# Layer norm roots by one power instruction on GpSimd in place of ten DVE steps, in a gated two-layer mixture kernel

## What is computed

```
def _layernorm(x, eps=1e-05):
    m = jnp.mean(x, axis=-1, keepdims=True)
    v = jnp.var(x, axis=-1, keepdims=True)
    return (x - m) / jnp.sqrt(v + eps)

x = x + tanh(g_xattn) * xattn(_layernorm(x), token_ids, ctx)   # 4 experts by token id
x = x + tanh(g_ffn)   * ffn(_layernorm(x), gate_w, W1, W3, W2, Ws1, Ws3, Ws2)  # 16 experts, top 2, and a shared one
```

## Time and profile before

| what | value |
|---|---|
| median of 3 runs | 550.39 us |
| lowest and highest | 548.08 and 554.18 us |
| profiled execution, span from first to last instruction | 549.1 us |
| busy: PE, DVE, ACT, POOL | 470.2, 350.1, 254.1, 241.3 us |
| stage 1 ends (last scatter of norm rows issued) | about 175 us into the span |

### The profile page before, as it was taken

How to read it: one execution, slowest core, us unless ns; L and a number is a source line. 1 busy time by engine, 2 the same in 40 slices (tenths; PEclk the granted TensorE clock), 3 DMA queues, 4 the chain that set the end, 5 groups by cost and what they waited for, 6 DMA issues and landing times.

```text
span 549.1 us, 9055 instructions
## 1 busy us (share of the span) xinstructions
PE 470.2 (86%) x2774; PEld 407.9 (74%) x2775; DVE 350.1 (64%) x766; ACT 254.1 (46%) x381; POOL 241.3 (44%) x266
## 2 busy tenths in 40 slices
PE   1058999999982899999996599999999999999980
PEld 1046778888871688887784599999999999998960
DVE  6657999899986245304689986666655656556520
ACT  4323445554434135425331366666655556555520
POOL 0645455555431000150035735556666666663442
PEclk9999999999996699999998699999999999999995
DMA  8317344444441821661034488888888988886453
GB/s 288 127 29 274 113 135 153 155 166 156 134 155 42 292 76 54 227 202 55 1 97 134 134 271 250 251 251 247 245 237 243 247 246 239 253 240 169 97 64 51
DMA packets 28665, 93.32 MB, mean 170 GB/s; under 512 B 4448, under 2 KB 4448, under 8 KB 28128
## 3 DMA queue, kind: packets, MB, share of 16 engines
q1 hardware_dynamic: 15696, 57.87, 32.1%
q0 software_dynamic: 12944, 35.14, 25.0%
HBM read 71.49 MB, written 23.07 MB: 172 GB/s over the span
## 4 chain that ended last, share of the span: by engine, by line
PE 42%; DMA 26%; DVE 11%; POOL 9%; issue 8%; ACT 1%; POOLq 1%; SPq 0%; DVEq 0%; ACTq 0%
PE psG L989 25%; DMA out<-ys,cur 22%; PE psY L989 12%; POOL out L410 4%; PE psT L994 4%; POOL cur L332 4%; DMA front<-in_x,cur 2%; DMA xh<-xh_sb,cur 1%; DVE nwt L756 1%; DVE front L898 1%; DMA cst<-in_const 1%; DVE qhot L900 1%; DMA ht<-xh,cur 1%; DVE stats L726 1%; DVE nwt L764 1%
## 5 line engine op out<-in xcount | busy, mean ns | idle before, releaser
L989 PE MATMUL psG<-bl,slot 128*128 128x256 f32 (+1 forms) x720 | 106.7, 308 | 1.9 <-DVE bl L791 1.4
L989 PEld LDWEIGHTS psG<-bl,slot 128*128 128x128 f32 x720 | 97.8, 193 | 9.5 <-DVE bl L791 1.8
L989 PE MATMUL psY<-arena 128*128 (+1 forms) x372 | 93.3, 402 | 3.1 <-DVE arena L717 3.1
L332 POOL COPY cur<-idx 128x1 int32 (+1 forms) x121 | 50.4, 416 | 102.0 <-DMA out<-ys,cur 30.5
L989 PEld LDWEIGHTS psY<-arena 128*128 128x128 f32 x372 | 69.0, 191 | 17.4 <-issue 3.8
L410 POOL DMA_INDIRECT out<-ys,cur x32 | 63.1, 1972 | 26.6 <-POOL cur L332 18.2
L989 PEld LDWEIGHTS psG<-bl,arena 128*128 128x128 f32 x576 | 71.9, 196 | 3.5 <-DVE bl L942 2.9
L989 PE MATMUL psG<-bl,arena 128*128 128x256 f32 x576 | 72.5, 288 | 2.1 <-DVE bl L942 2.1
L989 PE MATMUL psY<-slot,arena 128*128 128x512 f32 x288 | 71.2, 401 | 0.0
L780 DVE TENSOR_TENSOR slot<-raw,slot 128x1536 fp32r<-128x1536 f32 x27 | 47.3, 1760 | 33.7 <-ACT slot L474 19.5
L389 POOL TENSOR_TENSOR xh_sb<-ys,xb 128x512 f32<-128x512 f32 x16 | 24.2, 1523 | 100.1 <-ACT ys L516 88.3
(11 more groups left out here) (165 smaller groups left out, 602.9 us busy)
## 6 DMA issues: line engine op xcount, KB each, us to landing
raw<-in_w SPq DMA_DIRECT2D x51, 768.0 KB
ht<-xh SPq DMA_DIRECT2D x16, 256.0 KB, 2.9
xb<-xh SPq DMA_DIRECT2D x16, 256.0 KB, 2.9
out<-xh_sb SPq DMA_DIRECT2D x16, 256.0 KB, 2.0
raw<-in_ctx_t SPq DMA_DIRECT2D x2, 1024.0 KB, 8.5
ht<-in_ctx_t SPq DMA_DIRECT2D x1, 1024.0 KB, 12.2
xh_sb<-in_ctx_t SPq DMA_DIRECT2D x1, 1024.0 KB, 15.3
out<-log_sb SPq DMA_DIRECT2D x2, 256.0 KB, 14.0
```

The costliest lines, as they stand in the source:

```text
L332: pool.tensor_copy(cur[:, n:n + 1], table[:, bass.ds(q, 1), col]).then_inc(done, 1)
L989: ins = pe.matmul(ps, left[a], right[b], start=n == 0 and m == 0, stop=n == total - 1 and m == 2)
```

## The change

The root is taken by one instruction on GpSimd, `pow` of (var + eps) with a tile of constants -0.5. DVE keeps V (now var + eps), hands it to GpSimd by `var_ready`, and takes R back by `root_ready`. The wait for R and B stand behind `gate` and `low_h` in DVE's step. In GpSimd's list the power stands between the gather of xb and the gather of xa, with the two waits (`h_ready`, `xh_ready`) that keep R from being overwritten while ACT reads it.

```
         nwt = sb("nwt", [P, 5, 2])
+        half = sb("half", [P, 2])
...
             pool.memset(zeros[:, :], 0.0).then_inc(zeroed, 1)
+            pool.memset(half[:, :], -0.5).then_inc(half_set, 1)
...
             low_ctx(E1 - 2)
 
+            pool.wait_ge(half_set, 1)
+
             def step(t, par, known):
                 if have(known, 0):
...
                     pool.indirect_dma_start(xb[:, par, :], None, x, i).then_inc(xb_here[par], 16)
+                one, two = have(known, 2), have(known, -2)
+                if one or two:
+
+                    cs = slice(0 if one else 1, 2 if two else 1)
+                    pool.wait_ge(var_ready, t + 3)
+                    if had(known, 2):
+                        pool.wait_ge(h_ready, t + 2)
+                    if had(known, -2):
+                        pool.wait_ge(xh_ready, t - 2)
+                    pool.tensor_tensor(nwt[:, 3, cs], nwt[:, 0, cs], half[:, cs], ALU.pow).then_inc(root_ready, 1)
                 if have(known, 4):
...
-                    V, Y, T, R, B = (nwt[:, m, cs] for m in range(5))
-                    nw(dve.tensor_scalar(V, mv[:, cs, 1], EPS, 0.5, ALU.add, ALU.mult))
-                    nw(dve.tensor_scalar(Y.bitcast(I32), V.bitcast(I32), -0.5, float(0x5f3759df - (1 << 22) - (1 << 31)),
-                                         ALU.mult, ALU.add))
-                    for m in range(3):
-                        nw(dve.tensor_tensor(T, V, Y, ALU.mult))
-                        nw(dve.tensor_tensor(T, T, Y, ALU.mult))
...
-                        nw(dve.scalar_tensor_tensor(R if m == 2 else Y, T, -1.5, Y, ALU.add, ALU.mult))
-                    assert n[0] == NEWTON
-                    dve.scalar_tensor_tensor(B, mv[:, cs, 0], -1.0, R, ALU.mult, ALU.mult).then_inc(norm_ready, 1)
+                    V, R, B = (nwt[:, m, cs] for m in (0, 3, 4))
+                    dve.tensor_scalar(V, mv[:, cs, 1], EPS, None, ALU.add).then_inc(var_ready, 1)
                 if have(known, 0) and known != 0:
                     gate()
                 if have(known, 1) and known not in (FIRST + 1, 0):
                     low_h()
+                if one or two:
+                    dve.wait_ge(root_ready, NORMS(k, known))
+                    dve.scalar_tensor_tensor(B, mv[:, cs, 0], -1.0, R, ALU.mult, ALU.mult).then_inc(norm_ready, 1)
```

More of the change, by code:

```diff
@@ L182, in gated_layer @@
         xh_sent = [sem(f"xh_sent{n}") for n in range(2)]
-        stats_done, mv_done, newton, norm_ready = (sem(n) for n in ("stats_done", "mv_done", "newton", "norm_ready"))
+        stats_done, mv_done, var_ready, root_ready, norm_ready = (
+            sem(n) for n in ("stats_done", "mv_done", "var_ready", "root_ready", "norm_ready"))
+        half_set = sem("half_set")
         h_ready, hT_ps, hT_hi, hT_lo = (sem(n) for n in ("h_ready", "hT_ps", "hT_hi", "hT_lo"))
@@ L683, in _ @@
             dve.wait_ge(tg_ready, 1)
-            NEWTON = 11
             def step(t, par, known):
```

## The result

The changed kernel takes 567.59 us (median of 4 runs, 566.39 to 568.64), the kernel before 551.25 us in the runs beside it (median of 4). The ratio is 1.029, with a 95% interval of 1.025 to 1.033: slower by about 16 us, and the change touches only stage 1, whose last scatter ends at 189 us. The forecast was 565.5 us. The profiled execution spans 564.4 us, where the sum for it said 564.2, and took 566.39 us.

The account below looks back on a forecast made before the run. TensorE was taken to bound stage 1, with POOL nearly as full; the change closes a loop through POOL. Stage 1 ends 15.1 us later: 549.1 + 15.1 = 564.2 us, plus 1.3 for the median, 565.5 us; range 556 to 590.

Parts of the forecast that it names:

- the sum: Whole kernel: profiled span 549.1 us plus 15.1 us from stage 1 gives 564.2 us; 1.3 us more for the median.
- The bound before: Stage 1 loop: TensorE bounds at 6.50 us a step; POOL's list is taken for 5.98 us of it.
- the 0.14 us of slack: Stage 1 loop: TensorE needs 6.36 of 6.50 us a step, all that a lighter DVE could give back.
- The closed loop: Stage 1 loop: POOL waits each step for its power's way round; 7.27 + P, 7.92 us instead of 6.50.
- P: Duration of the power on POOL: 0.65 us, the geometric middle of 0.27 and 1.52 us.
- The start: Stage 1, t = -2 to 2: POOL's list is the chain; norm of t = 2 at 55.05 us, 1.3 earlier.
- The loop and its exit: From the norm of t = 2: 13 rounds, 103.0 us, then 6.7 us; norm of t = 16 17.4 us late.
- The end: Last steps of stage 1: x1 of t = 19 16.3 us late, root gains 1.2; stage 1 ends 15.1 late.
- The long power: Rival, POOL's power: as long as an accumulating DMA, 1.97 us; 29.0 us more, 594.5 us; 17%.
- The hidden power: Rival, between POOL's last DMA and next copy: the power costs no list time; 546.5 us; 7%.
- TensorE's clock: Rival, stage 1 loop: pauses lower the clock, 11.2 us a step, 43 us more, 608.5 us; 4%.
- A one-time stall: Rival, first power at t = -2: 2.0 us more, 567.5 us; 571.5 by the Trainium skill; 6%.

Follow-up runs that it names:

- without the ten steps: Kernel before with the root left out: DVE sets R to var + eps in one instruction, POOL takes no part; 545.95 us, ratio 0.988.
- the two powers: Changed kernel with the power done twice, the first time into a spare column; 582.54 us, ratio 1.051 to the kernel before.
- the quick operation: Changed kernel with a product by 1.0 in place of the power, same place and waits; 558.27 us, ratio 1.009 to the kernel before.
- the ten steps with one copy: Kernel before, DVE's ten root steps kept, with one copy of three index columns a step on POOL instead of three; 551.29 us, ratio 0.997.
- the power first: Changed kernel with the power moved ahead of the gather of xb in POOL's step; 553.06 us, ratio 0.999 to the kernel before.

## Why the prediction was right

**The bound before.** TensorE by the chain, POOL nearly as full by its timeline. Right: without the ten steps the loop went from 6.51 to 6.37 us and no further, as the 0.14 us of slack said.

**The closed loop.** Right in its form and nearly in its size: 7.92 us forecast, 8.05 measured. The difference is P and the pairs. P was put at 0.65 us and is 0.74 with two columns, 0.57 to 0.60 with one. No row had a power: 0.65 was the middle of two ends a factor of 5.6 apart, and that it came within 0.09 us is in part luck. The three pairs take 6.06 us instead of 5.98. The estimated hand-over from POOL to DVE was 0.05 and is 0.04 us (109.32 + 0.74 to 110.10).

**The start.** The norm of t = 2 begins at 54.18 us; the forecast was 55.05. Five powers of 0.58 us or 0.74 us instead of 0.65 are 0.2 of it. POOL's large addition is over at 27.91 us instead of 28.20, 0.3, and the hand-overs around a power take about 0.24 us instead of 0.30, another 0.3.

**The loop and its exit.** The norms of t = 15 and 16 begin at 158.61 and 165.26 us (forecast 158.0 and 164.7), the late x1 of t = 19 at 177.56 us (forecast 177.2). Two errors of opposite sign meet here: the start came 0.9 us early, and the 13 rounds took 104.4 us instead of 103.0.

**The end.** Stage 1's last norm begins at 185.95 us, 14.1 us late; the forecast was 15.1. The late x1 is 16.7 us late instead of 16.3. The root there goes from V at 184.91 to the norm at 185.95, 1.04 us, as forecast (1.12). What differs is the product before it. These are rows of the end, in the timeline of the changed kernel:

```profile
177.56 0.75 DVE L710 SCALAR_TENSOR_TENSOR xh_sb<-psY,tg,xb 128x512 f32<-128x512 f32 x1
...
179.79 2.98 PE L983 MATMUL psY<-arena 128*128 x12 [2.28 <-DVE arena L731]
...
183.11 0.75 DVE L710 SCALAR_TENSOR_TENSOR xh_sb<-psY,tg,xb 128x512 f32<-128x512 f32 x1 [1.67 <-DMA xh<-xh_sb,cur]
...
184.91 0.15 DVE L757 TENSOR_SCALAR nwt<-mv 128x1 f32<-128x1 f32 x1
185.15 0.57 POOL L375 TENSOR_TENSOR nwt<-nwt,half 128x1 f32<-128x1 f32 x1 [0.70 <-DVE nwt L757]
...
185.95 0.81 ACT L463 ACTIVATE xh_sb<-xh_sb,nwt 128x512 f32<-128x512 f32 x1 [3.65 <-DVE nwt L764]
```

Here twelve matmuls take 2.98 us. In the kernel before the same group began at 163.08 us and took longer:

```profile
163.08 4.60 PE L989 MATMUL psY<-arena 128*128 x12 [1.81 <-DVE arena L717]
```

That is 1.6 us which the forecast carried over. About 0.3 us of it is given back: the product is over at 182.77 us, and x1 begins at 183.11, since it then waits for the scatter DMA of the slot that it writes. So x1 follows x1 after 5.55 us instead of 6.85, 1.3 us less, and that is the error of the end. The busy times of the two groups, before and then after, in the columns of the earlier trace rows, tell what the 1.6 us are:

```profile
163.08:167.70 4.62, 4.60 (x12) 3.18 (x12) 1.88 (x12) 0.81 (x1) 0.60 (x2) 0.63 0.26 103
```

```profile
179.79:182.80 3.01, 2.98 (x12) 2.18 (x12) 0.30 (x2) 0.82 (x1) 1.60 (x3) 1.00 0.44 174
```

The granted clock fell in the group before: 0.63 on average and 0.50, the lower level, from 164 to 167 us. It didn't fall in the changed kernel. The change isn't shown to be the cause. In all traces but that of the changed kernel and that of the two powers this group starts after the same 1.81 us of idle time. It took 4.5 to 4.6 us at 0.63 in three of these nine (the kernel before, the quick operation, the ten steps with one copy) and 3.0 us at 1.00 in the other six. Rows 5 couldn't tell this.

**The sum.** 14.1 us come from stage 1. From the last norm to the end it is 378.5 us (564.4 - 185.95) against 377.3 before (549.1 - 171.83): 1.2 us more in stages that the change doesn't touch. Over all traces but that of the two powers, which has 381.3, the same stretch is 377.0 to 380.4 us, so 1.2 is within what it varies by. The agreement of 564.2 with 564.4 us is thus partly luck: 1.0 us too much in stage 1 and 1.2 too little behind it. The median was forecast from the span plus 1.3 us, and that is the larger part of the 2.1 us by which 565.5 is low: the changed kernel's profiled run has 2.0 us between span and time (566.39 - 564.4), and the median is another 1.2 us above it.

**The rivals.** The long power: no, 0.74 us. The hidden power: no, POOL's list holds it in full, and the second power adds another 0.67 us a step. TensorE's clock: no, 1.00 in the loop with 83% busy (13.27 of 16 us). Where it did fall, with two powers, it was for single groups of 4.6 us, and the step stayed at 8.72. A one-time stall: no. The first power takes 0.58 us, like the other one-column powers, and it begins at 27.86 us, where the addition ahead of it ends (23.41 + 4.50 us), so no hidden time stands before it either. The 6 us that the Trainium skill has for a first call of newly loaded code (GPSIMD Engine Reference, Instruction dispatch) don't appear for this operation.

## What to carry to other kernels

Before a result is moved to another engine, write down that engine's list and look at what stands directly behind the new instruction: if it waits, by way of other engines, for that very instruction, its list is closed into a loop whose length is the whole list plus the way round, however short the instruction is. Put the instruction ahead of work that needs nothing from it, and the way round is covered; here that is the difference between 567.6 and 553.1 us. And judge an engine's room by its timeline, not by its busy share: POOL showed 7 of 13 us busy and had 0.5 us a step to give.

## What the hardware showed that was not expected

- The power on GpSimd is cheap: 0.57 us for one column of 128, 0.74 for two, where a product of the same form takes 0.21 us for two. A further column thus costs 0.17 us or so.
- An indirect DMA begins 0.78 to 0.92 us after the end of the index copy ahead of it, but only 0.30 us after another indirect DMA whose wait is already met. So over half of the pause belongs to the copy and the wait for it, which one copy for three DMAs pays once. What the rest of the pause is, no run shows.
- The granted clock can fall in one kernel and not in the next after the same pause. The last group of psY took 4.60 us at 0.63 in the kernel before and 2.99 us at 1.00 with the power first, in both with TensorE busy for 6.19 of the 8 us ahead of it and idle for the last 1.81. In the changed kernel the pause was longer, 2.28 us, and the clock stayed at 1.00.
- In the loop of the two powers single groups of psY ran at the lower clock (4.6 us) after pauses of 1.3 to 1.6 us. In the changed kernel groups after 1.57 and 1.16 us of idle time took 3.0 us.

Whether DVE itself could take the power was not tried.
